# A quantised gated FFN on one core: the gate product stored as f32 and scaled later, its codes kept as magnitudes, and the sign put onto the up projection in the down stage

## The reference, cut to what matters

```python
x = x + ffn(x @ W[cat] + b[cat])             # (32, 128, 512): 4096 rows; one of 64 matrices W per batch of 128 rows

def ffn(x):                                  # hidden 512, inner 1536; the w_* are block-quantised to 4 bits
    x    = act_qdq(x)
    up   = act_qdq(x @ w_up.T)
    gate = act_qdq(x @ w_gate.T)
    sig  = clip(round(sigmoid(gate) * 65536), 0, 65535) / 65536
    gate = act_qdq(gate * sig)               # "the gate product", its codes are the act codes
    o    = act_qdq(gate * up)
    return o @ w_down.T

def act_qdq(x):                              # 16 bits, one scale for the whole tensor
    scale = max(max(abs(x)) / 32767, 1e-12)
    return clip(round(x / scale), -32768, 32767) * scale
```

## Time and profile before

| | us |
|---|---|
| median of 3 runs | 1051.67 |
| lowest, highest run | 1049.72, 1051.81 |
| span of the profiled execution, first to last instruction | 1048.0 |
| lowest run less the span (the page gives no whole time of the profiled execution itself) | 1.7 |
| median less the span | 3.7 |
| TensorE matmul busy | 903.8 (86%) |
| VectorE, ScalarE, GpSimd busy | 673.3, 466.6, 142.2 |

### The profile page before, as it was taken

How to read it: one execution, slowest core, us unless ns; L and a number is a source line. 1 busy time by engine, 2 the same in 40 slices (tenths; PEclk the granted TensorE clock), 3 DMA queues, 4 the chain that set the end, 5 groups by cost and what they waited for, 6 DMA issues and landing times.

```text
span 1048.0 us, 14250 instructions
## 1 busy us (share of the span) xinstructions
PE 903.8 (86%) x4904; PEld 486.8 (46%) x4904; DVE 673.3 (64%) x718; ACT 466.6 (45%) x487; POOL 142.2 (14%) x89
## 2 busy tenths in 40 slices
PE   6999989999999999999999988900007999999998
PEld 6999984444444444444444433400003444444443
DVE  0456779565575644499998588788898475545530
ACT  1113432433324333597887666659993132112100
POOL 0000000000000000343332577640000000000000
PEclk9999999999999999999999999955557999999999
DMA  8998962322432222899994455668865285555521
GB/s 285 380 374 288 302 222 94 124 115 118 170 161 91 120 90 91 303 377 380 391 364 199 144 172 179 213 225 293 319 228 171 89 296 167 173 178 158 175 77 60
DMA packets 66324, 218.96 MB, mean 209 GB/s; under 512 B 5811, under 2 KB 5811, under 8 KB 66291
## 3 DMA queue, kind: packets, MB, share of 16 engines
q1 hardware_dynamic: 56914, 168.05, 46.1%
q10 hardware_dynamic: 9376, 50.48, 12.0%
HBM read 148.38 MB, written 70.12 MB: 208 GB/s over the span
## 4 chain that ended last, share of the span: by engine, by line
PE 58%; issue 15%; DVE 15%; POOL 5%; ACT 3%; DMA 3%; DVEq 0%; ACTq 0%; SPq 0%; POOLq 0%
PE bank L695 10%; PE bank L779 8%; PE bank L780 8%; PE bank L781 8%; PE bank L745 7%; PE bank L746 7%; PE bank L747 7%; DVE act_codes L1101 3%; POOL pcode L478 2%; DVE tile_max L962 2%; DVE junk L1076 2%; DVE sigq L1069 2%; PE wt_bank L706 1%; PE bank L683 1%; POOL sig_int L482 1%
## 5 line engine op out<-in xcount | busy, mean ns | idle before, releaser
L779 PE MATMUL bank<-wt_down,o_parts 128*128 128x512 f16 x384 | 146.5, 382 | 113.0 <-DVE o_parts L1200 113.0
L547 ACT ACTIVATE stage<-bank 128x512 f32<-128x512 f32 x192 | 111.1, 591 | 166.2 <-PE bank L747 153.8
L780 PE MATMUL bank<-wt_down,o_parts 128*128 128x512 f16 x384 | 146.6, 382 | 0.0
L781 PE MATMUL bank<-wt_down,o_parts 128*128 128x512 f16 x384 | 146.4, 381 | 0.0
L745 PE MATMUL bank<-xq_head,wt_gate 128*128 (+1 forms) x336 | 128.1, 381 | 4.3 <-DVE xq_head L949 4.3
L745 PE MATMUL bank<-xq_head,wt_up 128*128 x336 | 128.0, 381 | 3.9 <-ACT stage L547 3.9
L746 PE MATMUL bank<-xq_head,wt_up 128*128 x336 | 128.1, 381 | 0.0
L746 PE MATMUL bank<-xq_head,wt_gate 128*128 (+1 forms) x336 | 128.0, 381 | 0.0
L747 PE MATMUL bank<-xq_head,wt_up 128*128 x336 | 128.0, 381 | 0.0
L747 PE MATMUL bank<-xq_head,wt_gate 128*128 (+1 forms) x336 | 127.9, 381 | 0.0
L962 DVE TENSOR_REDUCE tile_max<-stage 128x1 f32<-128x1536 f32 (+1 forms) x62 | 108.3, 1747 | 26.5 <-ACT stage L547 25.7
(11 more groups left out here) (119 smaller groups left out, 1272.5 us busy)
## 6 DMA issues: line engine op xcount, KB each, us to landing
w_ring<-in_L_cond_W_dram SPq DMA_DIRECT2D x32, 1024.0 KB, 7.3
gate_scratch<-stage ACTq DMA_DIRECT2D x32, 768.0 KB, 3.3
gate_ring<-gate_scratch SPq DMA_DIRECT2D x32, 768.0 KB, 8.0
up_scratch<-stage ACTq DMA_DIRECT2D x32, 768.0 KB, 5.9
up_again<-up_scratch SPq DMA_DIRECT2D x32, 768.0 KB, 4.8
up_head<-up_scratch SPq DMA_DIRECT2D x20, 768.0 KB, 6.2
gate_code_scratch<-code_ring SPq DMA_DIRECT2D x29, 384.0 KB, 5.6
code_ring<-gate_code_scratch SPq DMA_DIRECT2D x29, 384.0 KB, 3.1
```

The costliest lines, as they stand in the source:

```text
L547: nc.scalar.activation(stage[:, q % 2, n % PIECE_TILES, :], psum[n % BANKS][:, :], ACT.Copy)\
L779: nc.tensor.matmul(psum[r][:, :], o_hi, wt_down[:, 0, k, :], start=(k == 0), stop=False)
L780: nc.tensor.matmul(psum[r][:, :], o_hi, wt_down[:, 1, k, :], start=False, stop=False)
L781: return nc.tensor.matmul(psum[r][:, :], o_lo, wt_down[:, 0, k, :], start=False, stop=(k == NT - 1))
```

## The change: what it does

- Max pass: 5, 5, 5, 5, 6, 6 pieces in up chunks 0 to 5, starting with gate piece 4 (the last four are 0 to 3). The first four gate pieces are loaded during the gate stage. ScalarE rounds gate to codes, makes the sigmoid, and the magnitude of every second piece; VectorE makes the other magnitudes. The fused multiply-and-maximum writes its product (code magnitude x integer sigmoid) as f32 to a ring of four slots, from which SP stores 23 of the 32 to `product_scratch`; the last 9 stay in SBUF. GpSimd has only the `partition_all_reduce` of the scales left.
- Act pass, in up chunks 6 and 7 (0, 0, 0, 3 / 4, 4, 4, 4 / 4, 4, 4, 1): one VectorE operation per piece, f32 product times k_p to int16 magnitude. The 23 stored products are loaded again through six slots.
- Product stage: the act codes are magnitudes already, so the fused product and maximum reads them as they stand. The maxima have a column for each piece, and the merges between are gone.
- Down stage: each up piece comes with the gate piece of the same number, and a new VectorE operation sets up ^ (gate & 0x80000000), so the up codes carry the sign of gate. The operation for piece n + 1 stands ahead of the o codes of piece n. SP reloads a slot once ScalarE has made its up codes (before: once VectorE had used these).

```diff
-FIRST_STEPS, LOOP_STEPS = 8, 6
-ACT_STEPS = (11, 10, 10)
+PASS1 = (5, 5, 5, 5, 6, 6)
+LEAD = 4
+RING = 4
+SPILLED = 23
+KEPT = PIECES - SPILLED
+AHEAD = 6
+PASS2 = ((0, 0, 0, 3), (4, 4, 4, 4), (4, 4, 4, 1))
+MSLOTS = 4
-    gcode_dram = nc.dram_tensor("gate_code_scratch", (PIECES, P, PIECE), i16, kind="Internal").ap()
+    prod_dram = nc.dram_tensor("product_scratch", (SPILLED, P, PIECE), f32, kind="Internal").ap()
...
+        def due(count, at, of):
+            return -(-(at + 1) * count // of) + -at * count // of
...  SP
+            sp.wait_ge(w_scaled, 3 * WSLICES)
+            for j in range(RING):
+                load_gate(j)
+            for j in range(PIECES - RING):
+                sp.wait_ge(code_made, j + 1)
+                load_gate(j + RING)
+                if 1 <= j <= SPILLED:
+                    store_product(j - 1)
+            for k in range(SPILLED):
+                sp.wait_ge(product_out[k % RING], 16 * (k // RING) + 16)
+                if k < RING:
+                    sp.wait_ge(code_made, PIECES - RING + k + 1)
+                elif k < AHEAD:
+                    sp.wait_ge(sigq_made, PIECES - AHEAD + k + 1)
+                else:
+                    sp.wait_ge(act_made, KEPT + k - AHEAD + 1)
+                sp.dma_start(back_ring[:, k % AHEAD, :], piece_rows(prod_dram, k)).then_inc(back_in[k % AHEAD], 16)
+            for n in range(PIECES - 2):
+                if n < AHEAD:
+                    sp.wait_ge(act_made, PIECES - AHEAD + n + 1)
+                else:
+                    sp.wait_ge(umag_made, 2 + n - AHEAD + 1)
+                sp.wait_ge(stage_out[n % Q % 2], stored(n, 1))
+                sp.dma_start(up_ring[:, up_slot(n), :], piece_rows(up_dram, n)).then_inc(up_in[up_slot(n)], 16)
             def load_again(n, q):
                 sp.dma_start(up_again[:, q % 2, :], piece_rows(up_dram, n)).then_inc(up_again_in[q % 2], 16)
+                sp.dma_start(gate_again[:, q % 2, :], piece_rows(gate_dram, n)).then_inc(gate_again_in[q % 2], 16)
...  SP, finish_chunk, once per output tile
-                        used = held(sp, Q * i + Q + r + 1)
+                        used = held(sp, Q * i + Q + r + 2)
-                        sp.wait_ge(prod_used, used)
-                        load_again(Q * i + Q + r + 2, r)
+                        sp.wait_ge(ucode_made, used)
+                        load_again(Q * i + Q + r + 3, r + 1)
                     made = held(sp, BPC * i + r + 1)
                     sp.wait_ge(y_made, made)
...  ScalarE, after each copied up tile where due()
+                        if due(count, n, NT):
+                            if j + 1 < PIECES:
+                                gate_code(j + 1)      # waits for mag_vector or mag_scalar of piece j - 1
+                            sigmoid(j)
+                            if j % 2 == 0:
+                                code_magnitude(j)
+                            j += 1
...  ScalarE, product stage
-                    if v in MAG_SLOT:
-                        act_magnitude(USLOTS * turn + v, MAG_SLOT[v])
+            for k in range(PIECES):
+                up_magnitude(k)
...  VectorE
+            def max_step(j):
+                V.tensor_scalar(sigq[:, :], sig[:, j % 2, :], 65536.0, 65535.0, ALU.mult, ALU.min)
+                if j % 2:
+                    code_magnitude(j)                 # two operations, the second sets mag_vector
+                V.tensor_tensor_reduce(product_at(j), cmag[:, j % 2, :], sigq[:, :], 1.0, 0.0, ALU.mult, ALU.max,
+                                       p_max[:, j:j + 1]).then_inc(product_made, 1)
+            def act_step(m):
+                V.tensor_scalar(act_piece(n), src, k_p, None, ALU.mult).then_inc(act_made, 1)
...
+            def product_max(k):
+                V.tensor_tensor_reduce(junk[:, k % 2, :], act_piece((k - 2) % PIECES), umag[:, k % MSLOTS, :], 1.0, 0.0,
+                                       ALU.mult, ALU.max, o_max[:, k:k + 1]).then_inc(max_used, 1)
+            def signed_up(i, q):
+                for loaded in (up_again_in[q % 2], gate_again_in[q % 2]):
+                    dve.wait_ge(loaded, 32 * i + (16 if q < 2 else 32))
+                V.scalar_tensor_tensor(out=up_again[:, q % 2, :].bitcast(i32), in0=gate_again[:, q % 2, :].bitcast(i32),
+                                       scalar=-2 ** 31, in1=up_again[:, q % 2, :].bitcast(i32),
+                                       op0=ALU.bitwise_and, op1=ALU.bitwise_xor).then_inc(sign_made, 1)
```

More of the change, by code:

```diff
@@ L638, in magnitudes @@
-            def magnitudes(turn, first):
-                for v in range(USLOTS):
-                    used, loaded = held(act, USLOTS * turn + v + 3 - MSLOTS), held(act, 16 * turn + 16)
-                    act.wait_ge(scale_ready, R_UP)
-                    act.wait_ge(up_in[v], loaded)
-                    if not first or v + 3 > MSLOTS:
-                        act.wait_ge(max_used, used)
-                    up_magnitude(up_slot(v), (v + 2) % MSLOTS)
-                    if v in MAG_SLOT:
-                        act_magnitude(USLOTS * turn + v, MAG_SLOT[v])
@@ L649, in _, with gate_code @@
-            act.wait_ge(step_done, 2 * PIECES)
-            act_magnitude(PIECES - 1, MAG_SLOT[USLOTS - 1])
-            act.wait_ge(scale_ready, R_UP)
-            for k in range(2):
-                up_magnitude(stage[:, k, :, :].rearrange("p t c -> p (t c)"), k)
-            magnitudes(0, True)
-            with act.Fori(1, (PIECES - 2) // USLOTS) as turn:
-                magnitudes(turn, False)
+            def gate_code(j):
+                act.wait_ge(scale_ready, R_GATE)
+                act.wait_ge(gate_in[j % RING], 16 * (j // RING) + 16)
+                if j >= 2:
+                    act.wait_ge(mag_vector if j % 2 else mag_scalar, j // 2)
+                nc.scalar.activation(code[:, j % 2, :], gate_ring[:, j % RING, :], ACT.Copy, scale=k_g)\
+                    .then_inc(code_made, 1)
@@ new lines, in sigmoid, with code_magnitude @@
+            def sigmoid(j):
+                act.wait_ge(code_made, j + 1)
+                if j >= 2:
+                    act.wait_ge(sigq_made, j - 1)
+                nc.scalar.activation(sig[:, j % 2, :], code[:, j % 2, :], ACT.Sigmoid, scale=s_g)\
+                    .then_inc(sig_made, 1)
+            def code_magnitude(j):
+                act.wait_ge(code_made, j + 1)
+                if j >= 2:
+                    act.wait_ge(product_made, j - 1)
+                nc.scalar.activation(cmag[:, j % 2, :], code[:, j % 2, :], ACT.Abs).then_inc(mag_scalar, 1)
@@ new lines, in _, with up_magnitude @@
+            assert j == PIECES
+            def up_magnitude(k):
+                if k < 2:
+                    src = stage[:, k, :, :].rearrange("p t c -> p (t c)")
+                else:
+                    act.wait_ge(up_in[up_slot(k - 2)], 16 * ((k - 2) // AHEAD) + 16)
+                    src = up_ring[:, up_slot(k - 2), :]
+                if k >= MSLOTS:
+                    act.wait_ge(max_used, k - MSLOTS + 1)
+                nc.scalar.activation(umag[:, k % MSLOTS, :], src, ACT.Abs, scale=k_u).then_inc(umag_made, 1)
@@ L1218, in _, with down_pair @@
                 finish_tile(0, r, True)
-            with dve.Fori(1, CHUNKS // 2) as pair:
+            def down_pair(pair, last):
                 for h in range(2):
@@ L1222, in _ @@
                     for q in range(Q):
-                        product_codes(i, q, h, False)
+                        product_codes(i, q, h, False, last and h == 1)
                         finish_tile(i - 1, q, False)
+            with dve.Fori(1, CHUNKS // 2 - 1) as pair:
+                down_pair(pair, False)
+            down_pair(CHUNKS // 2 - 1, True)
             for r in range(BPC):
```

434 lines of the change are left out of this document (134 added, 300 removed).

## The result

| | before | after |
|---|---|---|
| median of 4 runs | 1050.70 us (1049.58 to 1051.81) | 1017.17 us (1015.60 to 1019.01) |
| profiled execution: time, span | as shown above | 1016.78 us, 1015.0 us |

The ratio is 0.9681 (95%: 0.9667 to 0.9696): 33.5 us faster. The forecast was 1014 with 1000 to 1032.

What follows compares the result with a forecast made beforehand. TensorE was taken as nearly full and bounding the down stage, with late act pass and product stage open before it. 1048.0 - 45 + 4 + 3.5 = 1010.5 us span; median 3.7 above, so 1014, range 1000 to 1032.

Steps and rivals of the forecast that it cites:

- Up stage and act pass: Before the product stage: TensorE's up stage ends at 668, not 680.3; up scale at 683 us, against 708 before.
- The 3 us that I added: Max pass, up chunks 4 and 5: ScalarE's gate code of odd pieces waits for VectorE's magnitude, putting product scale at 616.
- DMA as the limit: From 631 us, 54 transfers of 1.98 us bound act pass and product stage; last reduction at 743, 45 us earlier.
- the rival of VectorE's bound: Product stage: VectorE bounds it, DMA keeping 416 GB/s or more; last reduction at 737, 1005 us; chance 0.20.
- Sign operation and opening: Opening of the down stage: sign operation 1.8 us, load wait 2.3; first matmul 9.4 after the last reduction, +4.
- The price of a slot in the steady down stage: Rest of the down stage: VectorE's 5.8 us per slot hides under TensorE's 7.74; cost 0.
- The stops: the step that failed: Down stage: piece 8's load behind the first y tile stops TensorE 2.5 us, about 1 more next chunk; +3.5.
- the slow clock at the first matmul: Start of the down stage: 2.5 us lost to TensorE's slow clock.
- The sign of being right: Down chunk 1: a second wait of TensorE of 2 to 4 us at o codes would show the forecast right.
- The lockstep of the max pass: Max pass: ScalarE and VectorE alternate on every second piece, scale up to 13 us later; 1024 us; chance 0.17.
- The slow DMA: DMA transfers from 631 us on: 2.2 us each, giving 1026 us; chance 0.08.
- the down stage stayed TensorE's: Rival for the down stage: a sign operation over 3.8 us sets the slot; 1068 us at 5.5; chance 0.04.

Runs made afterwards that it cites:

- e6: Changed kernel, but from the 7th product on only half of each is stored and loaded again; ratio 0.9570 to the kernel before, span 1006.1 us.
- e7: Changed kernel, but from the seventh up piece of the product stage on only half of each is loaded; ratio 0.9641 to the kernel before, span 1010.5 us.
- e11: e10 plus two more products loaded ahead of the act pass, into memory of the x codes; median 1001.46 us, ratio 0.9534 to the kernel before.
- e5: Changed kernel with VectorE finishing the first y tile one piece earlier, SyncE's row unchanged; median 1012.08 us, ratio 0.9625 to the kernel before.
- e1: Changed kernel with SyncE's down-stage loads of up and gate pieces issued further ahead; median 1009.09 us, ratio 0.9618 to the kernel before.
- e4: Changed kernel with both down-stage loads kept but no sign operation, ScalarE waiting for the loads itself; ratio 0.9553 to the kernel before, span 1002.6 us.
- e2: Changed kernel with the edits of e1 and e5 together; median 1008.60 us, ratio 0.9616 to the kernel before.
- e10: e2 plus each of the first four down-stage loads leaving when its own slot is free; median 1007.42 us, ratio 0.9597 to the kernel before.
- e9: Changed kernel with ScalarE making every code magnitude in the max pass, VectorE none; median 1019.48 us, ratio 0.9701 to the kernel before.

## Why the prediction was right, and which terms were off

The mechanism was right at its large steps. Two terms of the sum were mis-sized, the transfers and the stops, and one, the slow clock behind a stop, was missing.

| step | predicted | measured |
|---|---|---|
| TensorE's up stage ends | 668 | 668.9, no stop |
| end of the product's scale chain | 616 | 618.4 |
| up scale | 683 | 682.2 |
| last reduction | 743 | 739.98 |
| to the first down matmul | +9.4 | +9.5 |
| stops in the down stage | 3.5 | 8.7 |
| slow clock after the long stop | not in the sum | 2.1 |
| span | 1010.5 | 1015.0 |

- *Up stage and act pass.* Right. TensorE's 12 us and the late act pass are gone (first window above). The scale of the product came 2.4 us later than I had it. Of this 0.9 is a slip in my addition: 606.3 + 5.8 + 1.8 is 613.9 and not 613. The 3 us that I added for ScalarE waiting on VectorE's magnitude had the right reason and were 1.5 too few: of the last four pairs three took 11.5 us and one 10.9, against the plan's 10.3. It did not reach the end: among the ten act codes lay two maxima and not three (621.22 and 626.59), and the train of loads began at 631.2, as forecast.
- *DMA as the limit.* Right, and shown by e6, e7 and e11. The size was 3 us off: ScalarE had the last up piece at 736.3, so the 54 transfers counted from 633 took 1.91 us each, not 1.98. The windows above have 410 and 422 GB/s, and the pitch of 1.88 us in the product stage is 418. The page "DMA: Bandwidth & Descriptors" of the Trainium skill puts the bound between HBM and SBUF at about 358 GB/s in "Where 436 GB/s comes from", and its section "Measured" has 425. The trace does not bear out the first and is near the second. So the forecast and the rival of VectorE's bound lay closer together than I had them: about 2 us (e7), not 6.
- *Sign operation and opening.* 1.8 taken, 1.75 measured; the opening within 0.1 us. The price of a slot in the steady down stage is nothing, as forecast: no stops after the first two, 465 matmuls in 100 us.
- *The stops: the step that failed.* I named the place, the loads of piece 8 behind the first y tile, and priced it as load + sign - ScalarE's share = 2.5 (the terms add up to 2.2), and 1 in the next chunk. That part was right: from the issue of the loads to the finished o codes of piece 7 it took 11.7 us (785.93 to 797.63) against 9.4 before, 2.3 more. What I left out is that the loads themselves left 6.5 us later. My sum took the y tile to come 27.8 us after the first matmul, as before (821.17 - 793.33). There it had waited 3.94 us for TensorE; VectorE was ready 23.9 us after the first matmul. Now seven sign operations stand before the tile in VectorE's row, nearly 12 us, and 2.8 us of waits for gate loads, where there had been 3.7 us of waits for ScalarE. The tile comes 34.35 us after the first matmul, 6.5 later. Together 8.8 us, against 8.7 of stops: 1.65 for the tile itself, whose PSUM bank TensorE needed, and 7.07 for the o codes. I had VectorE's 5.8 us of work per slot against TensorE's 7.74 and called it spare; but at the opening VectorE works slots ahead, in the order of its row, and the urgent tile stands behind pieces that TensorE needs only later. e5 (the tile moved) and e1 (the load moved) each take that apart.
- *The clock.* The granted clock fell to half speed (0.50) at 795.0, inside the long stop, and rose at 801.9, 4.2 us after TensorE had started again; the 0.81 from 800 to 805 above is the mean of both levels. Half of 4.2 is 2.1 us, and the down stage is 10.8 us longer than before, of which 8.7 are stops. I had charged the slow clock at the first matmul and forgot that a new stop can bring it again:

```profile
798.00:800.00 2.00, 2.00 (x6) 0.76 (x5) 0.94 (x2) 0.00 (x0) 0.00 (x0) 0.50 0.32 120
```

- *From span to median.* I took 3.7 us; here the median is 2.2 above the profiled span.

The balance: 1010.5 - 3.0 + 0.1 + 5.2 + 2.1 = 1014.9 against a span of 1015.0. That the median came within 3.2 us of the forecast is partly luck: -3.0 for the reduction and -1.5 from span to median stood against +7.3 in the down stage. The sign of being right that I had given for that stage, one second wait of 2 to 4 us, did not appear; there were two waits, 1.65 and 7.07.

Of the rivals, VectorE as the bound is the nearest miss. The lockstep of the max pass happened, but the scale came 4.5 us behind the plan where that rival had up to 16. The slow DMA did not happen, and the down stage stayed TensorE's.

## What to carry to other kernels

When an operation is added to an engine with slack per step, ask what stands behind it in that engine's row and in the queue that waits for it: the slack is an average, and the cost falls at the first place where a load waits for a product of that row. Look there for a load that can be issued one buffer earlier; here it was four lines in a queue's order and gave back 6.6 us of median by the ratios. Price a stop of TensorE with the slow clock that can follow it. When the compute of a stage is removed, multiply out its bytes: the transfers were the next limit, with the engine behind them only 2 us away.

## What the runs showed of the hardware

- A full f32 output costs VectorE's fused product nothing (1.758 against 1.756 us for 128 x 1536), and a bitwise operation of two int32 inputs costs the same 1.75 as the fused product of two 16-bit inputs.
- The same fused product took 1.76 us with GpSimd idle and 2.42 to 2.78 where it overlapped a rounding by GpSimd (all eleven such cases in the max pass of the kernel before, and none of the other 21).
- A down stage is about 252.3 us of work (252.1 to 252.6 in all 13 profiles), plus TensorE's stops, plus half of the time that TensorE then ran at a granted clock of 0.50. All in us:

| | stops | at half speed after the first matmul | at half speed after a stop | down stage |
|---|---|---|---|---|
| before | 0 | 4.9 | 0 | 254.7 |
| e4 | 0 | 2.7 | 0 | 253.4 |
| e2 | 1.20 | 5.4 | 0 | 256.1 |
| e1 | 1.98 | 4.4 | 0 | 256.5 |
| e10 | 2.11 | 3.9 | 3.4 | 258.1 |
| e5 | 4.49 | 4.6 | 5.2 | 261.6 |
| changed | 1.65 + 7.07 | 4.6 | 4.2 | 265.5 |
| e9 | 3.96 + 4.54 | 5.2 | 5.0 + 5.6 | 268.7 |

- The length of a stop alone does not tell whether the clock falls. It fell after 2.11 us in e10, but not after 2.47 in e6 (its first stop) or after 1.98 in e1, and after every stop of 3.96 us or more. The row after e1's stop, which ended at 783.85:

```profile
790.00:800.00 10.00, 10.00 (x48) 4.47 (x47) 5.02 (x5) 1.58 (x1) 0.00 (x0) 1.00 0.87 295
```

- Transfers of 0.786 MB, loads with a few stores between, ran at 410 GB/s over 33 us beside a full TensorE, and at 422 over the next 14 beside a nearly idle one.
- Back-to-back activations of 128 x 1536 are recorded with 1.57 us and start 1.47 apart: 589.03 and 590.50 for a sigmoid and the copy behind it. A sum of recorded durations puts ScalarE's work too high.
